# A second series of scatters for the base rows, gathers moved into the last pairs, and zeros in TensorE's pauses

## The reference

```python
x = x + attn(layernorm(x))        # recurrence per head; 'out' is nonzero in every third token only
# ffn, on h = layernorm(x):
logits = h @ w_router.T
top_idx = top_k(logits, 1)
scores = sigmoid(logits) * one_hot(top_idx)
gate, up = split(einsum('eth,ehf->etf', scores * h, gate_up_proj))
expert_out = einsum('etf,efh->eth', up * silu(gate), down_proj)
shared = silu(h @ w_gate.T) * (h @ w_up.T) @ w_down.T
x = x + shared + expert_out.sum(0)
```

## Time and profile before

| | |
|---|---|
| median of 3 runs | 586.87 us (586.18 to 588.09) |
| the profiled execution | 586.47 us |
| its span in the trace | 584.4 us |
| PE, DVE busy | 508.2 us (87%), 465.3 us (80%) |
| ACT, POOL busy | 275.5 us (47%), 391.3 us (67%) |
| mean granted clock of PE | 0.969 |

### The profile page before, as it was taken

How to read it: one execution, slowest core, us unless ns; L and a number is a source line. 1 busy time by engine, 2 the same in 40 slices (tenths; PEclk the granted TensorE clock), 3 DMA queues, 4 the chain that set the end, 5 groups by cost and what they waited for, 6 DMA issues and landing times.

```text
span 584.4 us, 7030 instructions
## 1 busy us (share of the span) xinstructions
PE 508.2 (87%) x1845; PEld 270.5 (46%) x1845; DVE 465.3 (80%) x782; ACT 275.5 (47%) x579; POOL 391.3 (67%) x401
## 2 busy tenths in 40 slices
PE   3799989999999999888788798889999997839993
PEld 2544434455554434344355465545554254515562
DVE  4889999998999999999788797589999978423331
ACT  3567645455545545322354266545455416604341
POOL 3289788878787878866687333446776867474554
PEclk9999999999999999999999699999999997959998
DMA  6910125930000477000441113310100002143440
GB/s 173 209 47 18 36 69 150 306 76 1 1 0 1 109 267 235 1 1 1 107 128 38 45 56 101 81 45 20 36 29 18 1 5 55 61 146 86 113 117 0
DMA packets 42410, 43.63 MB, mean 75 GB/s; under 512 B 4776, under 2 KB 35622, under 8 KB 41992
## 3 DMA queue, kind: packets, MB, share of 16 engines
q1 hardware_dynamic: 38212, 36.66, 23.3%
q0 software_dynamic: 3120, 6.09, 3.6%
q10 hardware_dynamic: 1040, 0.43, 0.3%
HBM read 24.79 MB, written 19.37 MB: 76 GB/s over the span
## 4 chain that ended last, share of the span: by engine, by line
PE 60%; DVE 17%; issue 8%; POOL 6%; ACT 6%; DMA 2%; POOLq 0%; SPq 0%; DVEq 0%; ACTq 0%
PE ps L2238 11%; DVE grown L1696 6%; PE ps L2255 5%; PE ps L2187 5%; PE ps L2197 5%; PE ps L2188 5%; POOL grown L1293 4%; DVE ps L1730 3%; PE ps L2295 3%; PE ps L1952 3%; PE ps L2298 3%; PE ps L2296 3%; PE ps L2174 2%; PE ps L2245 2%; PE ps L2162 2%
## 5 line engine op out<-in xcount | busy, mean ns | idle before, releaser
L1696 DVE TENSOR_TENSOR grown<-ps,steps 128x1536 f32<-128x1536 f32 x64 | 112.1, 1752 | 1.7 <-ACT ps L859 0.2
L1293 POOL TENSOR_TENSOR grown<-grown 128x512 f32<-128x512 f32 x64 | 80.6, 1268 | 41.3 <-DVE grown L1718 40.7
L2187 PE MATMUL ps<-grown,cst 128*128 128x512 f32 x128 | 68.5, 617 | 12.3 <-DVE grown L1696 11.9
L2238 PE MATMUL ps<-steps 128*128 x128 | 70.7, 651 | 5.2 <-issue 4.1
L1038 ACT ACTIVATE uv<-ps 128x512 f32<-128x512 f32 x64 | 38.1, 596 | 64.7 <-DVE grown L1718 64.4
L1172 POOL TENSOR_TENSOR uv<-uv,steps 128x512 f32<-128x512 f32 x64 | 67.5, 1075 | 0.0
L2188 PE MATMUL ps<-grown,cst 128*128 128x512 f32 x128 | 65.4, 593 | 0.0
L2197 PE MATMUL ps<-uv,cst 128*128 128x512 f32 x128 | 60.4, 594 | 0.5 <-POOL uv L1172 0.5
L1381 POOL TENSOR_TENSOR early<-state,qT 128x512 f32<-128x512 f32 x22 | 37.7, 1712 | 32.2 <-DVE state L1710 32.2
L1582 DVE TENSOR_TENSOR e_h<-rk,ps 128x256 f32<-128x256 f32 x64 | 25.5, 418 | 40.8 <-PE ps L2245 20.6
L1718 DVE TENSOR_TENSOR grown<-ps,steps 128x512 f32<-128x512 f32 x64 | 43.5, 680 | 5.3 <-PE ps L2187 4.7
(11 more groups left out here) (256 smaller groups left out, 1034.2 us busy)
## 6 DMA issues: line engine op xcount, KB each, us to landing
steps<-gate_up_proj SPq DMA_DIRECT2D x1, 4096.0 KB, 14.8
slot_rows<-no_row SPq DMA_DIRECT2D x1, 3469.5 KB, 16.0
steps<-slot_rows SPq DMA_DIRECT2D x13, 257.0 KB, 3.5
xs_others<-zeros SPq DMA_DIRECT2D x1, 2496.0 KB, 10.9
steps<-xs_others SPq DMA_DIRECT2D x19, 128.0 KB, 2.2
ys_others<-e_y SPq DMA_DIRECT2D x19, 128.0 KB, 1.8
early<-chain_m SPq DMA_DIRECT2D x4, 512.0 KB, 5.9
xf<-x SPq DMA_DIRECT2D x4, 495.0 KB
```

Source lines behind the costliest of these rows:

```text
L1293: G.tensor_tensor(decayed[:, h], decayed[:, h], work[:, h, 1], ALU.add).then_inc(s_add[h], 1)
L1696: V.tensor_tensor(grown[:, :, h].rearrange("p e (x w) -> p e x w", w=HD), st, per_col(tile, FF, 3, h, HD), ALU.mult).then_inc(s_prod[h], 1)
L2187: T.matmul(bank[2 * h + 1], c["block"], work[:, h, 1], start=True, stop=True).then_inc(s_usum[h], 1)
L2238: T.matmul(b_gu(run, b)[u], e_xT[:, b, u], gu[:, bass.ds(ex * (2 * F), 2 * F)], start=True, stop=True).then_inc(s_eg, 1)
```

## The change

- `slot_rows` gets rows of 129 floats (scaled row and token number), and a new DRAM tensor `slot_bases` takes the base rows of 128 floats. POOL scatters the 11 tiles of the first as soon as they are scaled, and then in a second series of 11 scatters the base rows, as the groups of the shared expert end.
- SP loads the first four pairs' rows, waits for all base scatters, loads all bases in three DMAs (4, 10 and 12 tiles) into the new `e_base`, and then the rows of pairs 4 to 12. A load of rows no longer waits for `add_base` of the pair four before, but for its transposes.
- Of the eight gathers behind the mixed scatters, four stay there and one each goes behind the sends of pairs 0 to 3. The others' last rows are added behind pair 8 (before: pair 1), and all 20 stores of the others' rows come in a row behind that, and behind all loads.
- The conversion of the token numbers goes from POOL to DVE, ahead of `add_base`.
- In `shared(MIXED)` ACT scales all 11 tiles ahead of the second SiLU of group 0 (it did 4, 4 and 3 in the three groups). DVE computes the slots ahead of the second half of group 0's product. PE computes the ranks behind all four products of group 0.
- PE multiplies tiles of zeros (`keep_busy`) into free banks of PSUM at seven places.
- The DMAs of Wout and ln_w count on the semaphore of the feed-forward weights, so what waited for five DMAs waits for seven; two semaphores of the second norm are merged with those of the first.
- The volume written to zero the slots at about 107 us stays the same and is now in two DMAs.

```diff
@@ -735,7 +742,7 @@
             def load_rows(k):
                 b = k % DEEP
                 if k >= DEEP:
-                    sp.wait_ge(s_eo, k - DEEP + run.g0 + 2)
+                    sp.wait_ge(s_et, k - DEEP + run.g0 + 1)
                     sp.wait_ge(s_to, k - DEEP + 1)
                 sp.dma_start(e_row[:, b], x_in[:, k * U:(k + 1) * U, :]).then_inc(s_row[b], 16)
 
@@ -756,14 +763,16 @@
             stores = [(b, part) for b in range(B) for part in range(5)]
             for k in range(DEEP):
                 load_rows(k)
-            for k in range(2, run.n):
-                if k + 2 >= DEEP and k + 2 < run.n:
-                    load_rows(k + 2)
-                if k == 3:
-                    sp.wait_ge(s_fin, 3)
-                if k >= 3:
-                    for b, part in stores[2 * k - 6:2 * k - 4]:
-                        store_others(b, part)
+            sp.wait_ge(s_based, 16 * MIXED.n)
+            for part in range(3):
+                lo, hi = BASE_PARTS[part:part + 2]
+                sp.dma_start(e_base[:, lo:hi], slot_bases.rearrange("(m p) d -> p m d", p=P)[:, lo:hi, :]
+                             ).then_inc(s_base[part], 16)
+            for k in range(DEEP, run.n):
+                load_rows(k)
+            sp.wait_ge(s_fin, 3)
+            for b, part in stores:
+                store_others(b, part)
             sp.wait_ge(s_out, 16 * 5 * B)
             for k in (0, 1):
                 sp.wait_ge(s_sent[k], 16 * U * ((run.n + 1 - k) // 2))
...
@@ -979,32 +988,35 @@
...
+                for g in range(len(t.groups)):
                     if t is OTHERS:
                         shared_rows(t, g)
                         if g == 0:
                             scaled_rows(t, 0, 4)
-                    for k in (0, 1):
-                        act.wait_ge(s_fgu, 2 * n + k + 1)
-                        if n or k:
-                            act.wait_ge(s_fh, 2 * n + k)
-                        S.activation(f_silu[t.name][:, 0:w], b_gate[k][:, 0:w], ACT.Silu).then_inc(s_fsg, 1)
+                    silus(g, 0)
+                    if t is MIXED and g == 0:
+                        mixed_rows(NW - 1)
+                        score(t)
+                        S.activation(fb[t.name]["token"], c["token_mixed"], ACT.Copy).then_inc(s_sc, 1)
+                        scaled_rows(t, 0, t.n)
+                    silus(g, 1)
                     if t is OTHERS:
                         scaled_rows(t, 4 * g + 4, 4 * g + 8)
                         if g == 0:
                             piece(1)
                         if g % 2:
                             piece(2 + g // 2)
-                    else:
-                        if g == 0:
-                            mixed_rows(NW - 1)
-                        if g + 1 < len(t.groups):
-                            shared_rows(t, g + 1)
-                        if g == 0:
-                            score(t)
-                            S.activation(fb[t.name]["token"], c["token_mixed"], ACT.Copy).then_inc(s_sc, 1)
-                        scaled_rows(t, lo, hi)
+                    elif g + 1 < len(t.groups):
+                        shared_rows(t, g + 1)
             act.sem_inc(s_uc[0], 1)
             act.sem_inc(s_uc[1], 1)
 
...
@@ -1385,31 +1402,25 @@
             gather(OTHERS, 0, AHEAD, 0)
             q, run = fb[MIXED.name], RUNS[2]
 
-            def tokens(k):
-
-                b = k % DEEP
-                pool.wait_ge(s_row[b], 16 * (k // DEEP + 1))
-                G.tensor_copy(e_to[:, k], e_row[:, b, :, D]).then_inc(s_to, 1)
-
-            pool.wait_ge(s_xz, 48)
+            pool.wait_ge(s_xz, 64)
             pool.wait_ge(s_idx, 2)
+            for j in range(MIXED.n):
+                scatter_tile(MIXED, j)
             for g, (lo, hi) in enumerate(MIXED.groups):
                 pool.wait_ge(s_fa, GA[MIXED.name] + g + 1)
                 for j in range(lo, hi):
-                    scatter_tile(MIXED, j)
-            gather(OTHERS, AHEAD, OTHERS.n, 1)
-            tokens(0)
-            tokens(1)
+                    scatter_base(j)
+            gather(OTHERS, AHEAD, AHEAD + 4, 1)
 
             for k in range(run.n):
-                if k + 2 < run.n:
-                    tokens(k + 2)
                 pool.wait_ge(s_to, k + 1)
                 pool.wait_ge(s_eo, k + run.g0 + 2)
                 for u in range(U):
                     G.indirect_dma_start(out_rows, bass.IndirectOffsetOnAxis(ap=e_to[:, k, u:u + 1].bitcast(U32), axis=0),
                                          e_y[:, k % 2, u], None, bounds_check=B * N - 1, oob_is_err=False
                                          ).then_inc(s_sent[k % 2], 16)
+                if AHEAD + 4 + k < OTHERS.n:
+                    gather(OTHERS, AHEAD + 4 + k, AHEAD + 5 + k, 1)
 
         @block.vector
         def _(dve):
...
@@ -1548,6 +1558,7 @@
                 link(V.tensor_tensor(r_a, r_a, oh, ALU.mult))
                 link(V.tensor_reduce(q["slot"], r_a, AX.X, ALU.add))
                 V.tensor_tensor(q["idx"][:], q["slot"], c["spare_" + t.name], ALU.add).then_inc(s_idx, 1)
+                shared_h(t, 0, 1)
                 shared_add(t, 0)
 
                 te = q["r_te"][0:1].rearrange("p (m e) -> p m e", e=E)
...
@@ -1903,18 +1914,28 @@
                     dve.wait_ge(s_sent[b], i * (8 * U) + 16 * U * (k // 2))
                 else:
                     dve.wait_ge(s_ew[b], 16 * (1 + run.base[b]))
-                V.tensor_tensor(e_y[:, b], b_y(run, b).rearrange("p (u d) -> p u d", u=U), e_row[:, k % DEEP, :, D + 1:], ALU.add
+                part = next(n for n in range(3) if k * U < BASE_PARTS[n + 1])
+                dve.wait_ge(s_base[part], 16)
+                V.tensor_tensor(e_y[:, b], b_y(run, b).rearrange("p (u d) -> p u d", u=U), e_base[:, k * U:(k + 1) * U], ALU.add
                                 ).then_inc(s_eo, 1)
+
+            def tokens(k):
+
+                b = k % DEEP
+                dve.wait_ge(s_row[b], 16 * (k // DEEP + 1))
+                V.tensor_copy(e_to[:, k], e_row[:, b, :, D]).then_inc(s_to, 1)
 
             def pair(i, k, ahead):
                 if ahead:
                     gate(RUNS[2], i, k + 1, (k + 1) % 2)
+                tokens(k)
                 add_base(i, k)
-                if k == 1:
+                if k == run.n - 5:
                     dve.wait_ge(s_gat[1], 16 * (OTHERS.n - AHEAD))
                     others_out(AHEAD, OTHERS.n)
 
-            over_pairs(RUNS[2], pair)
+            run = RUNS[2]
+            over_pairs(run, pair)
 
         @block.tensor
         def _(pe):
...
@@ -2161,10 +2184,12 @@
                             pe.wait_ge(s_fh, 2 * n + k - 1)
                         T.matmul(b_gate[k][:, 0:w], wT[:, k], xT_shared(t, g), start=True, stop=True)
                         T.matmul(b_up[k][:, 0:w], wT[:, 2 + k], xT_shared(t, g), start=True, stop=True).then_inc(s_fgu, 1)
-                        if t is MIXED and (g, k) == (0, 0):
-                            rank(t)
+                    if t is MIXED and g == 0:
+                        rank(t)
                     if g + 1 < len(t.groups):
                         transposes(g + 1)
+                    elif t is OTHERS:
+                        keep_busy(5, 2, HALF)
                     pe.wait_ge(s_fh, 2 * n + 2)
                     if n:
                         pe.wait_ge(s_fa, n)
@@ -2174,6 +2199,11 @@
                             ins = T.matmul(b_tok[:, at:at + D], f_h[t.name][:, k, at:at + P], wT[:, 4 + k], start=(k == 0),
                                            stop=(k == 1))
                     ins.then_inc(s_fy, 1)
+
+            def keep_busy(b, n, w):
+
+                for _ in range(n):
+                    T.matmul(bank[b][:, 0:w], c["block"], zeros[:, 0:w], start=True, stop=True)
 
             for h in (0, 1):
                 pe.sem_inc(s_ba[h], 1)
@@ -2284,6 +2314,7 @@
 
 
             shared(OTHERS)
+            keep_busy(3, 2, HALF)
             pe.wait_ge(s_bc, 2)
             pe.wait_ge(s_fa, NOG)
             pe.wait_ge(s_we, 48)
@@ -2380,11 +2411,14 @@
             out_of(1)
             centred(2)
             centred(3)
+            keep_busy(1, 1, HALF // 2)
             variances(VAR_HALF, L2)
             out_of(2)
             out_of(3)
+            keep_busy(1, 3, HALF // 2)
 
             shared(MIXED)
+            keep_busy(1, 2, HALF)
             pe.wait_ge(s_fa, GA[MIXED.name] + len(MIXED.groups))
             pe.wait_ge(s_idx, 2)
             pairs(RUNS[2])
```

More of the change, by code:

```diff
@@ L233, in build @@
         normed = nc.dram_tensor("normed", (B, N, D), F32).ap()
-        slots = nc.dram_tensor("slot_rows", ((MIXED.tiles + 1) * P, 2 * D + 1), F32).ap()
+        slots = nc.dram_tensor("slot_rows", ((MIXED.tiles + 1) * P, D + 1), F32).ap()
+        slot_bases = nc.dram_tensor("slot_bases", ((MIXED.tiles + 1) * P, D), F32).ap()
         out_rows = out.rearrange("b n d -> (b n) d")
@@ L487, in build @@
```

(10 more changed lines are left out.)

47 lines of the change are left out of this document (28 added, 19 removed).

## The result

| | before | changed |
|---|---|---|
| median of 17 runs each, us | 585.68 | 587.91 |
| profiled execution / its span, us | 586.47 / 584.4 | 589.06 / 587.3 |
| indirect DMAs that POOL issues | 81 | 92 |

What follows compares the result with a forecast made beforehand. PE was taken to bound the pairs, POOL and two DMA latencies the mixed tail. From 586.47 us, -1.7 + 0.0 + 2.3 - 0.9 + 0.1 = -0.2 gave 586.3 us; 8-in-10 range 582.8 to 588.9.

Steps and rivals of the forecast that it cites:

- zeros at the others' shared expert: Products of zeros in PE's pauses near 326 us keep its clock up: -1.7 us, bounds 0 and -2.4.
- rows of pair 4: Rows of pair 4, queued behind the base loads, come at 536.2 against 536.29 before: 0.0 us.
- half clock behind the pause: PE pauses 2.9 us in pair 2 and restarts at half clock: +2.3 us, bounds 0 and 2.7.
- the pairs' excess over 3.75 us: With stores gone from the first stretch of pairs, their 1.26 us excess shrinks: -0.9 us, range 0 to -1.3.
- the end: The 20 later stores land about as late as the last send: +0.1 us, range 0 to +1.5.
- the early rows: Rows for pairs 0 to 3 load 4.4 us sooner, but PE cannot use this.
- Rival 2: Loads overlap more than queue order suggests, pair 4's rows come by 533.3: 581.0 us in all; chance 0.09.
- the half clock that was forecast ahead of the first down product: In `shared(MIXED)`, after a 7 us pause, PE's 16 records take 4.1 us, the next gate product 1 us more.
- the rival of half clock all through the mixed part: PE stays at half clock through `shared(MIXED)`, done 8 us later: 589 to 590 us in all; chance 0.13.
- stretches of "5 to 7 us": Argument against half clock throughout `shared(MIXED)`: the clock came back after half-clock stretches of 5 to 7 us with similar pauses.
- all bases are in by 535.7: Base loads ahead of the pairs: 1.70 MB in 5.8 us, fixed part 2.0, gathers and sends 0.6, done by 535.7.
- the start: Fixed part of SP's base loads after the last scatter lands: 2.0 us (2.88 less 0.9).

Runs made afterwards that it cites:

- e14: Changed kernel plus ten products of zeros of 256 columns ahead of the transposes of pair 4: 586.78 us, 1.0006 of the kernel before.
- e13: Changed kernel with eight row buffers instead of four, rows of pairs 4 to 7 ahead of the base loads: 582.60 us, 0.9938 of the kernel before.
- e15: e13 with `add_base` of pair 0 later, others' last add behind pair 5, stores spread behind row loads 9 to 12: 584.35 us, 0.9972 of the kernel before.
- e17: Kernel before without its last 8 gathers and the add that uses them (73 indirect DMAs): 583.89 us, 0.9960 of the kernel before.
- e18: Kernel before with only the zeros at the others' shared expert added: 584.48 us, 0.9981 of the kernel before.
- e1: Same kernel as e18, run where the kernel before takes about 598 us: 596.54 us, 0.9978 of the kernel before.
- e5: Changed kernel as it is, a control where the kernel before takes about 598 us: 609.37 us, 1.0184 of the kernel before.
- e11: Same kernel as e13, run where the kernel before takes about 598 us: 610.36 us, 1.0186 of the kernel before.

## Why the prediction was wrong

The sum was -0.2 us, the two spans differ by +2.9. By its terms, from the rows above and the earlier trace rows:

| step | forecast | in the traces |
|---|---|---|
| zeros at the others' shared expert | -1.7 | 379.99 for 381.65: -1.66 (alone in time -1.1) |
| rows of pair 4 (PE's transposes) | 0.0 | 536.65 + 1.66 for 536.29: +2.0 |
| half clock behind the pause | +2.3 | 1.06 to `add_base` of pair 2 (2.44 for 1.38) and 0.97 in pairs 3 and 4 (8.47 for 7.50): +2.0 |
| the pairs' excess over 3.75 us | -0.9 | 0.81 left of 1.26 (27.06 us for 7 pairs): -0.45 |
| the end | +0.1 | 12.68 for 11.72 behind `add_base` of pair 11: +0.96 |
| sum | -0.2 | +2.9 |

**What held.** The mechanism: slots at 495.1 (forecast 495.3), first scatter 495.93 (496.2), last 523.17 (522.9), base loads issued at 525.45 (525.6), no use in the early rows, PE's pause in pair 2, and the clock behind it (e14). Rival 2's price for rows in time, 5.3 us under the forecast, is near the 5.6 that e13 took off the changed kernel, but partly by luck: the pause that went was 5.15 us and not 2.9, and e13 kept one of 2.12 with some half clock behind it. PEclk of 0.50 in 498 to 502 is the half clock that was forecast ahead of the first down product, and it was back at 1.00 from 506 us on, so the rival of half clock all through the mixed part didn't happen. (Of the stretches of "5 to 7 us" that spoke against it, the first was longer: in the kernel before PEclk is 0.50 to 0.53 from 326 to 336.)

**The step that failed** is the size of "all bases are in by 535.7 [...] So they come at 535.7 + 0.5 = 536.2", that is 534.5 in the changed kernel's trace, with the first term in it. They came at 536.61. From the last scatter's landing to the rows it took 11.2 us, not 8.9. The rate was right (288 GB/s in 530 to 536, 297 forecast), the bytes were not: the windows hold 0.76 + 1.73 = 2.49 MB from 526 to 536, of which 1.70 are bases and 0.13 the rows, and the other 0.66 are gathers and sends (nine of 64 KB each are on their way in that time). I had counted 0.4 MB for these and charged 0.6 us; 0.66 MB are 2.2 us at 297 GB/s, so 1.6 of the missing 2.3 us are theirs. The other 0.7 are the start, for which I had put 2.0: SP needed 3.06 us to issue the three loads, and 190 GB/s flowed in 526 to 530. This split is worked out from one trace; no run varied the bytes, and in e13 and e14 the three issues took 1.6 us. The pause then was 5.15 us and not 2.9. The order in the queue was read rightly, and e13 bears it out: the same load, ahead of the bases in the same queue, is there in time, and it took 8.00 us behind them. That agrees with the rule that the Trainium skill gives for a ring (DMA: Bandwidth & Descriptors, "Queues, rings and completion order"): a DMA engine takes its descriptors in their order.

**The end** was mis-sized by 0.9 us with the wrong cause. I looked for it in the stores, and these ended about with the last send, as forecast (SP is through at 582.3). e15 and e17 show the loss in POOL's drain, 81 ns for each of the 11 added scatters. Nothing in the prediction priced the number of indirect DMAs there.

**The pairs** gave half of what was forecast. From `add_base` of pair 4 (547.56) to that of pair 8 (562.88), with no store beside them, they took 3.83 us each; the three behind that (574.62 for pair 11), beside the stores, 3.91, where the kernel before took 3.75. What holds the first four above 3.75 was not looked into.

**The first term** has its -1.66 in the trace, but 1.1 us in time (e18); the traces of before and after were both a little slower than their medians.

The chance given to slower by over 0.3%, 0.16, was too small: nearly all its mass lay in one rival, while the sum's own errors (bytes 1.6, slow start 0.7, end 0.9) had one sign: a term too small, a start too quick, and an item left out.

## What to carry to other kernels

What one queue has ahead of an urgent small load must be counted in bytes with everything else that flows in that time, and a load that needs nothing of a long wait belongs ahead of the wait: here eight buffers instead of four turned a loss of 0.33% into a gain of 0.62%. A second series of indirect DMAs pays three times: its pitch of 1.27 us, what queues behind its end, and POOL's drain. When one wait is removed, look for the next on another engine before a further edit: behind the rows came the first bases (e13), and with these out of the way the stores among the row loads (e15).

## What the hardware showed that I had not expected

- POOL's last drain grows with the number of indirect DMAs that the whole program issued, far from the end too: 6.785 us at 73, 7.44 at 81, 8.34 at 92. Over all traces it is 7.41 to 7.45 at 81 and 8.25 to 8.35 at 92, so 73 to 85 ns each.
- A pause of 2.12 us of PE (e13) was followed by PEclk 0.57 in 530 to 534. In e14 one of 2.96 us was followed by 0.67 in 530 to 534, and the clock came back to 1.00 while ten products of zeros ran (4.85 us), though they wrote nothing that is used.
- The same kernels ran in a second condition, in which the kernel before took 13 us more and the changed one 21: engines that wait for PE's products went on 3 to 10 us after the records have them done (e1, e5, e11).
